# Graph network stack, layers 0 and 1: part of the layer norm on GpSimd, stores and loads on other queues, a new order of the row preparation

## The reference

```
layer 0: norm = d^-1/2 * adj.T * d^-1/2 (d = column sums of adj);  norm @ (h @ W0) + bias
layer 1: inc = adj + (adj > 0) / ||adj > 0||_row;  (inc @ h) / rowsum(inc)
layer 2: four attention heads, h @ W2; softmax(leaky_relu(src_i + dst_j) + adj), mean over the heads
layer 3: relu(adj @ (max(sign(h), 0) @ sign(W3).T))
```

## Time and profile before

| | |
|---|---|
| runs, median (lowest to highest) | 728.18 us (727.69 to 729.91) |
| the profiled execution | 727.12 us |
| its span, first to last instruction | 724.8 us |
| layer 0's products on PE | 65.6 to 149.5 us |
| layer 1's blocks on PE | 149.5 to 274.1 us |
| mean granted clock of PE | 0.995 |

### The profile page before, as it was taken

One profiled execution on the slowest core, in us unless ns is written; L12 is line 12 of the kernel. 1 busy time (PEld: TensorE's weight loads), 2 busy tenths in 40 slices (PEclk: granted clock), 3 DMA queues, 4 the chain that ended last, 5 costly groups with the idle time before them and its releaser, 6 DMA issues.

```text
span 724.8 us, 16131 instructions
## 1 busy us (share of the span) xinstructions
PE 691.0 (95%) x6480; PEld 586.1 (81%) x6480; DVE 629.4 (87%) x1161; ACT 472.4 (65%) x814; POOL 135.6 (19%) x162
## 2 busy tenths in 40 slices
PE   3998999986999999999999999999999999999998
PEld 3676888875888885468888888888888888888887
DVE  6898579688999854799999999989999899998683
ACT  3887153648887624886557867578766778667660
POOL 3962721301223220001210021200121000000000
PEclk9999999998999999999999999999999999999999
DMA  9997999677499887759988779997999831126791
GB/s 337 342 318 238 426 424 309 201 185 219 134 275 277 190 175 234 162 127 243 235 193 235 176 166 257 199 267 161 229 224 228 267 129 30 30 81 188 255 392 46
DMA packets 146457, 159.54 MB, mean 220 GB/s; under 512 B 90896, under 2 KB 103888, under 8 KB 141904
## 3 DMA queue, kind: packets, MB, share of 16 engines
q1 hardware_dynamic: 127328, 117.10, 53.7%
q0 software_dynamic: 19056, 41.42, 25.4%
HBM read 76.15 MB, written 52.46 MB: 177 GB/s over the span
## 4 chain that ended last, share of the span: by engine, by line
PE 60%; DVE 21%; ACT 6%; DMA 4%; issue 4%; SPq 2%; POOL 2%; ACTq 0%; DVEq 0%; POOLq 0%
PE ps L835 11%; PE ps L837 11%; PE ps L836 11%; DVE arena L1473 6%; PE ps L775 6%; DVE arena L1480 5%; PE ps L877 4%; PE ps L878 4%; DVE arena L1346 2%; DMA arena<-in_adj_dram 2%; SPq L383 2%; ACT arena L1003 2%; PE ps L719 2%; PE ps L721 1%; PE ps L720 1%
## 5 line engine op out<-in xcount | busy, mean ns | idle before, releaser
L835 PE MATMUL ps<-arena 128*128 128x257 f16 x1024 | 279.9, 273 | 1.0 <-DVE arena L1480 0.6
L837 PE MATMUL ps<-arena 128*128 128x257 f16 x1024 | 279.4, 273 | 0.0
L836 PE MATMUL ps<-arena 128*128 128x257 f16 x1024 | 279.2, 273 | 0.0
L1168 ACT ACTIVATE arena<-arena 128x512 f16<-128x512 f32 x252 | 158.3, 628 | 93.8 <-PE ps L837 56.3
L1473 DVE SCALAR_TENSOR_TENSOR arena<-arena,w_j 128x512 f32<-128x512 f32 x256 | 190.2, 744 | 0.0
L1480 DVE TENSOR_TENSOR arena<-arena 128x512 f16<-128x512 f32 x256 | 175.7, 687 | 8.1 <-ACT arena L1168 7.8
L835 PEld LDWEIGHTS ps<-arena 128*128 128x128 f16 x1024 | 99.9, 98 | 15.0 <-issue 1.4
L836 PEld LDWEIGHTS ps<-arena 128*128 128x128 f16 x1024 | 100.3, 98 | 12.5
L837 PEld LDWEIGHTS ps<-arena 128*128 128x128 f16 x1024 | 99.8, 97 | 12.9
L719 PE MATMUL ps<-arena 128*128 128x257 f16 x256 | 71.1, 278 | 1.9 <-DVE arena L1298 1.9
L721 PE MATMUL ps<-arena 128*128 128x257 f16 x256 | 70.5, 275 | 0.0
(11 more groups left out here) (154 smaller groups left out, 1154.9 us busy)
## 6 DMA issues: line engine op xcount, KB each, us to landing
adj_t<-arena POOLq DMA_DIRECT2D x32, 1024.0 KB, 7.9
arena<-in_adj_dram SPq DMA_DIRECT2D x32, 512.0 KB, 6.0
arena<-in_adj_dram SPq DMA_DIRECT2D x16, 1024.0 KB, 5.8
adj_parts<-arena SPq DMA_DIRECT2D x16, 1024.0 KB, 25.7
arena<-adj_t SPq DMA_DIRECT2D x64, 256.0 KB, 4.5
arena<-adj_t SPq DMA_DIRECT2D x16, 1024.0 KB, 6.7
x<-arena POOLq DMA_DIRECT2D x15, 512.0 KB, 5.7
arena<-u_rows SPq DMA_DIRECT2D x4, 1024.0 KB, 14.7
```

The source lines that it names most:

```text
L835: mm(ps[:, bank, 0:DE], hi, ht_hi[:, head, j, 0:DE], start=s, stop=False)
L836: mm(ps[:, bank, 0:DE], hi, ht_lo[:, head, j, 0:DE], start=False, stop=False)
L837: ins = mm(ps[:, bank, 0:DE], lo, ht_hi[:, head, j, 0:DE], start=False, stop=e)
L1168: nc.scalar.activation(p_hi[:, j % 4, :], prob[:, j % 4, :], copy).then_inc(p_hi_done, 1)
```

## The change

The diff, cut to its core (the lines of the new order are complete for SP, POOL, ACT and DVE in layers 0 and 1). `inc_slot` and the two functions after it only say which of three buffers a row uses; `wa_junk` gets eight buffers instead of four.

```diff
-        COUNTS = (1, 2, 9, 10, 11)
-        FILLS = (3, 4, 11, 12, 14)
-        HIGHS = (4, 7, 12, 13, 15)
-        LOWS = (5, 8, 13, 14)
+        COUNTS = (1, 2, 6, 7, 8, 11, 12)
+        FILLS = (3, 4, 8, 9, 11, 13)
+        HIGHS = (4, 6, 9, 10, 13)
+        LOWS = (5, 7, 10, 12, 14)
+        MAXIMA = 3
+        def inc_slot(t):
+            return t % 2 if t < 4 else (t - 2) % 3
...
@@ SP: while adj is read, after half 11
+                    sp.dma_start(b0_bc, b0_d.partition_broadcast(P)).then_inc(bias_in, 16)
...
             def reload_rows(t):
-                sp.wait_ge(filled, t - 2)
+                sp.wait_ge(filled, inc_last(t) + 1)
                 load_rows(t)
...
-            def turn_adj(n):
+            def turn_adj(n, part):
                 q, g = n // TG, n % TG
-                if n >= 2:
+                if n >= 2 and part == 0:
                     sp.wait_ge(wide[(n - 2) % TG], 16 * ((n - 2) // TG + 1))
...
-            sp.wait_ge(h0_lo_done, NB)
-            sp.dma_start(b0_bc, b0_d.partition_broadcast(P)).then_inc(bias_in, 16)
-            for k, (lo, hi) in enumerate(SENT):
-                for b in range(lo, hi):
-                    sp.dma_start(nat_dram[b * P:(b + 1) * P], ...).then_inc(nat_sent[k], 16)
+            reload_rows(2)
             reload_rows(3)
-            reload_rows(4)
             sp.wait_ge(y_ps, 6)
             sp.wait_ge(max_made, 7)
             sp.wait_ge(nat_sent[3], 48)
-            load_rows(2)
+            load_rows(4)
             sp.wait_ge(nat_sent[2], 32)
             turn_inc(0)
             sp.wait_ge(y_ps, 8)
+            sp.wait_ge(max_made, 9)
             turn_inc(1)
+            reload_rows(5)
+            reload_rows(6)
...
             for t in range(2, AHEAD):
-                reload_rows(t + 3)
                 sp.wait_ge(y_ps, 10 + t)
+                sp.wait_ge(max_made, 11 + t)
                 turn_inc(t)
-            for t in range(AHEAD + 3, 12):
-                reload_rows(t)
+                if t == 2:
+                    reload_rows(7)
+            reload_rows(8)
             for k in range(5):
                 sp.wait_ge(nat_sent[k], 16 * (SENT[k][1] - SENT[k][0]))
-            for n in range(2):
-                sp.wait_ge(inc_in[4 - n], 32)
-                turn_adj(n)
-            for t in range(12, NB):
-                reload_rows(t)
-            for n in range(2, QB):
-                turn_adj(n)
+            sp.wait_ge(inc_in[4], 32)
+            turn_adj(0, 0)
+            reload_rows(9)
+            turn_adj(0, 1)
+            sp.wait_ge(inc_in[3], 32)
+            turn_adj(1, 0)
+            reload_rows(10)
+            turn_adj(1, 1)
+            reload_rows(11)
+            reload_rows(12)
+            turn_adj(2, 0)
+            reload_rows(13)
+            turn_adj(2, 1)
+            reload_rows(14)
+            turn_adj(3, 0)
+            reload_rows(15)
+            turn_adj(3, 1)
...
@@ POOL
+            pool.wait_ge(bias_in, 16)
+            for t in range(NB):
+                pool.wait_ge(normed, t + 1)
+                nc.gpsimd.tensor_tensor(x[:, t, :], x[:, t, :], b0_bc, ALU.add).then_inc(bias_added, 1)
             pool.wait_ge(deg_copied, 1)
             ... dinv ...
-            (the same bias adds, after dinv)
             def inverse_root1(t):
+                pool.wait_ge(dl, CHAIN0 * (t + 1))
+                if t >= 2:
+                    pool.wait_ge(h1_lo_done, t - 1)
+                nc.gpsimd.tensor_scalar(ln_relu[:, t % 2, :], x[:, t, :], mean_var[:, t % 2, 0:1], 0.0, ALU.subtract,
+                                        ALU.max).then_inc(relu1, 1)
                 pool.wait_ge(ve1, t + 1)
                 ... power -1/2 ...
             def inverse_root2(t):
+                (the same for h2_relu, after dm and h2_lo_done)
...
                 inverse_root1(t)
-                if t in COUNTS:
-                    inverse_count(COUNTS.index(t))
+                if t - 1 in COUNTS:
+                    inverse_count(COUNTS.index(t - 1))
             for t in range(NB):
                 if t >= 1:
                     inverse_root2(t - 1)
-                if t + 5 < NB:
+                if 2 <= t and t + 5 < NB:
                     inverse_count(t + 5)
+                if t == 5:
+                    widen_high(0)
                 if t == 6:
-                    widen_high(0)
-                if t == 7:
                     add_low(0)
                     widen_high(1)
-                if t == 8:
+                if t == 7:
                     add_low(1)
-                if t == 11:
+                if t == 9:
                     widen_high(2)
-                if t == 12:
+                if t == 10:
                     add_low(2)
                     widen_high(3)
-                if t == 13:
+                if t == 11:
                     add_low(3)
...
@@ PE, layer 1
-                    if g == 3 and t == 6:
+                    if g == 3 and t == 15:
                         pe.wait_ge(wa_done, 1)
-                        for k in range(4):
+                        for k in range(NB - 2):
                             scores(k)
-                    if g == 3 and t >= 6:
-                        scores(t - 2)
...
@@ ACT
+            def send_nat(k):
+                lo, hi = SENT[k]
+                for b in range(lo, hi):
+                    nc.scalar.dma_start(nat_dram[b * P:(b + 1) * P], ...).then_inc(nat_sent[k], 16)
+            act.wait_ge(nat_lo_done, HALVES)
+            for k in range(2):
+                send_nat(k)
             ... g_hi of the 16 blocks ...
+            for k in range(2, 6):
+                send_nat(k)
...
             for t in range(NB):
                 h1_high(t)
+                if t in HIGHS:
+                    inc_high(HIGHS.index(t))
                 if t in COUNTS:
                     sign(COUNTS.index(t))
                     count(COUNTS.index(t))
-                if t in HIGHS:
-                    inc_high(HIGHS.index(t))
...                 (layer 1: sign and count from t = 2; part 3 now ahead of h2_high)
@@ DVE
+            dve.wait_ge(bias_added, NB)
             v.memset(nat_max, 0.0).then_inc(max_made, 1)
...             (layer0: no wait for bias_added, no subtraction L1323)
+            for t in range(MAXIMA):
+                maxima(t)
             for t in range(NB):
-                maxima(t)
+                if t + MAXIMA < NB:
+                    maxima(t + MAXIMA)
                 layer0(t)
...             (row_norm: no subtraction L1396)
-                if t == 0:
-                    inc_low(4)
-                if AHEAD <= t + 4 < NB:
+                if t == 1:
+                    fill(6)
+                if 3 <= t and t + 4 < NB:
                     fill(t + 4)
...
                 if t >= 1:
                     h2_low(t - 1)
-                (dot products in blocks 1 to 4, low part of W2 in blocks 5 to 8)
+                if t == 12:
+                    dve.wait_ge(w2_in, 32)
+                if t in (12, 13):
+                    w2_a(t - 12, range(HEADS))
+                if t == 14:
+                    w2_a_parts()
+                    dve.wait_ge(w2_hi_done, 1)
+                if t in (14, 15):
+                    (two of the four operations of L1435 in each)
-                if t == 12:
+                if t == 11:
                     dve.wait_ge(max_made, NB + 1)
                     v.tensor_reduce(amax[:, 0:1], nat_max, AX_X, ALU.max).then_inc(amax_part, 1)
```

More of the change, by code:

```diff
@@ L156, in gnn_stack @@
         w2_f = view(72 * KB, [DC, HD], F32)
-        wa_junk = view(80 * KB, [4, D], F32)
+        wa_junk = [view((80 + 57 * (k // 4) + k % 4) * KB, [D], F32) for k in range(2 * HEADS)]
         h2_t = view(H2T, [2 * DC, N], F16)
@@ L196, in gnn_stack @@
         SENT = ((0, 1), (1, 3), (3, 5), (5, 8), (8, 11), (11, NB))
+        CHAIN0 = 2
+        CHAIN1 = 3
         EARLY = 4
@@ L212, in gnn_stack, with inc_use, inc_last @@
         DINV_PIECES = ((0, 1), (1, 4), (4, 9), (9, NB))
+        def inc_slot(t):
+            return t % 2 if t < 4 else (t - 2) % 3
+        def inc_use(t):
+            return sum(inc_slot(k) == inc_slot(t) for k in range(t + 1))
+        def inc_last(t):
+            return max(k for k in range(t) if inc_slot(k) == inc_slot(t))
         def row_slot(t):
@@ L375, in turn_inc @@
                                            ).then_inc(inc_in[t % AHEAD], 16)
-            def turn_adj(n):
+            def turn_adj(n, part):
                 q, g = n // TG, n % TG
-                if n >= 2:
+                if n >= 2 and part == 0:
                     sp.wait_ge(wide[(n - 2) % TG], 16 * ((n - 2) // TG + 1))
                 slot = (turn_l1 if q == 0 else turn_l2)[n % 2]
[L382 to L385, removed]
+                sp.dma_start_transpose(out=slot[:, part, :, :],
+                                       in_=nat_dram[TG * P * g:TG * P * (g + 1), part, QB * P * q:QB * P * (q + 1)]
```

(19 more changed lines are left out.)

37 lines of the change are left out of this document (12 added, 25 removed).

## The result

| | us | ratio to before (95% interval) |
|---|---|---|
| before, median of 4 runs | 727.93 | |
| after, median of 4 runs (752.39 to 754.92) | 753.47 | 1.0347 (1.0319 to 1.0375) |
| predicted | 737.2 (723 to 747) | |

The account below looks back on a forecast made before the run. PE was taken to set the pace outside layers 0 and 1, where some 14 us could be won. Terms -2.3 -1.3 -3.0 +9.9 +2.6 +3.1 = +9.0 on 727.1 profiled gave 736.1, median 737.2 us (723 to 747).

Parts of the forecast that it names:

- seam and its half clock, to block 3: Between layers 0 and 1: block 2 starts 2.3 us earlier, and the half clock behind the seam is halved, -1.3.
- gaps of blocks 3 to 11: Layer 1: DVE loses the subtraction and the W2 work of blocks 1 to 8, so 3.0 us of gaps go.
- stops at the rows, half clock: Layer 1, block 9: row 13's read waits behind turn_adj(2, 0); PE stands 9.9 us, then half clock, +2.6.
- end of layer 1: Last turns of layer 1: late W2 work and POOL's subtraction make PE wait for W2, +3.1 us (+1.3 to +5.6).
- The loop itself: Layer 0's loop over 16 blocks through DVE, POOL and ACT: 5.65 us per block with a fill or split ahead.
- keeps 95.4 us as the time of block 3: Layer 0: block 3's statistics still end at 95.4 us, because ACT's first high part will not come before 85.33.
- the loop above hides even that: Layer 0: bias adds ahead of dinv may start it up to 5.8 us later, at no cost unless the seam closes.
- have this stop as cover: Layer 1: reads of rows 14 and 15, behind later turn_adj transfers, cost nothing beyond the stop at row 13.
- if POOL stands before `add_low(3)`: End of layer 1: upper bound of that term, +5.6 us against the +3.1 forecast.
- (a): Rival: row 13's stop doesn't come, the row or `wide` being there in time; 724.7 us, chance 0.14.
- (b): Rival: POOL's subtraction costs about what DVE's did, the seam closes, row 13's stop stays; 726.5 us, chance 0.16.
- (c): Rival: DVE's two-input operations shut POOL out; layer 0 starts 5.8 us late, loop 6 us a block; 751 us, chance 0.15.

Follow-up runs that it names:

- the last-but-one experiment: Kernel with rows first, subtraction on DVE and bias after dinv (717.2 us), but layer 1's subtraction on POOL again: 725.3 us, ratio 0.9944.
- the pause: Changed kernel with one wait added: in each block of layer 0 DVE waits after the variance until POOL's subtraction is done; 749.5 us, ratio 1.0263.
- the one with four parts undone: Changed kernel with rows read first, subtraction on DVE, bias after dinv and W2 work early: 718.5 us, ratio 0.9846.
- the other four: Rows first, subtraction on DVE, bias after dinv: 717.2 us; that with add_low(1) in block 8: 713.3; with layer 0's subtraction on POOL: 728.8; with layer 1's: 725.3.

## Why the prediction was wrong, step by step

The prediction's terms against the table of first products. The scores that moved (0.15 us for each block's six products, 1.6 us for the eleven that left earlier blocks, 2.0 forecast) are taken out of the blocks and of the end: +3.28 at block 3; gaps 0.9 less up to block 8 and the 1.6 us gap at 242 us gone; the stops 9.44 + 4.60 and 2.3 + 1.7 for the clock behind them; 25.96 - 17.13 - 1.6 at the end.

| term | forecast | measured | |
|---|---|---|---|
| seam and its half clock, to block 3 | -3.6 | +3.3 | failed |
| gaps of blocks 3 to 11 | -3.0 | -2.5 | right |
| stops at the rows, half clock | +12.5 | +18.0 | mechanism right, one stop missed |
| end of layer 1 | +3.1 | +7.2 | mechanism right, POOL's wait and half clock left out |
| sum | +9.0 | +26.0 | |

**The seam: the start of the loop.** The loop itself was right: from block 3 (100.07 us) to block 14 (162.40) it takes 5.67 us a block, 5.65 was forecast, and a subtraction behind a fill takes 3.3, forecast 2.3 + 0.9. (In four of the five blocks with a split it is the power that is held up, not the subtraction.) What failed is the sentence that keeps 95.4 us as the time of block 3 because ACT's first high part would not come sooner. The price of the bias adds stood beside it, up to 5.8 us (measured 5.80), and was dismissed with "the loop above hides even that". That sum put 5.8 us on PE's end of layer 0 alone. But the loop is fed by PE's first block: a late layer 0, with its half clock, delays the loop as well, and block 3 came 4.7 us late. ACT's stores, the reason that was given for 85.33, are issued behind the high parts of `g` and so come late with layer 0 too: ACT's first high part came at 89.27, and at 89.00 with the subtraction on DVE. The other failure is to have seen the adds and the subtractions as two edits. Both are POOL's: behind `dinv` the adds slow DVE, whose statistics the first subtraction needs (85.00 us), ahead of it they hold up layer 0. Only without the subtraction does moving them pay in full (8.6 against 1.5 us).

**The stops.** The first was right in place, chain and size: 9.44 us, forecast 9.9, from `add_low(0)` landing 7.7 us after its issue (8.7 forecast) and the row 6.1 after its own (5.8). The step that failed is "reads 14 and 15 stand behind `turn_adj(2, 1)` and `(3, 0)`, but have this stop as cover". The cover is 9.4 us; what row 14 lost was 6.12 us of SP and 13.7 us to land. Such a landing was in the rows (17.2 at most) and was left out as a matter of the stores; here none of those was in flight. It made a stop of 4.60 and twice the half clock: 2.3 + 1.7 us instead of 2.6. With the subtraction on DVE the second stop is 0.84 us, and the row lands in 10.6 us; whether POOL's subtraction slows the transfers was not separated.

**The end of layer 1.** The chain was right, and the larger bound (+5.6 "if POOL stands before `add_low(3)`") named what happened: POOL stood 5.23 us, DVE then 1.90 us for the high part, and layer 2's first product is 5.5 us late, the scores taken out. The forecast took this as a bound. The other 1.7 us are the half clock of layer 2's first twelve products, for which the sum had no term. It takes two things to make the end long, POOL's subtraction and the late W2 work: undoing the one gains 3.9 us there (4.4 by the last-but-one experiment), undoing the other 5.8 without the scores, and with the subtraction on DVE the W2 work may stand early or late. The sentence that POOL's subtraction in layer 1 "has cover" failed too: 3.7 us in blocks 0 to 10 once the covering losses are gone.

**The rivals.** (a) and (b) are out: the stops came, the subtraction cost 2.36 us in layer 0's mean. (c) was the case, at 0.15: POOL shut out, layer 0 5.8 us late, 751 against the median of 753.5. That its total came so close is in part luck: its loop of 6 us was too long, it hid the late start behind that loop, it had one stop for two, and it kept the small gaps, of which 2.5 us went. The argument against it, the median of 1.72 us, came from work that held up PE by 0.2 us in all; the duration that counts is the one at the moment when POOL's input is ready, which is when DVE starts its next long operation.

(c)'s rule, in the Trainium skill on SBUF — State Buffer, section SBUF: two separate sides, is an exclusive lock between GpSimd and a DVE instruction with two SBUF inputs: the one that starts first holds it for the whole instruction. This case agrees where DVE starts with POOL or before it: 3.31 us beside a fill of 2.35, 1.15 beside an operation that takes one input from PSUM, 1.15 throughout with the pause. Where POOL has started first it agrees in part: DVE's split pays 0.5 us beside a bias add (1.75 instead of 1.23), its maximum 0.2 beside a subtraction that it overlaps for 1.03 us, and the split that starts 0.65 us into a subtraction nothing (2.29, 2.28 in the mean with the subtraction on DVE). (b)'s rule, on the GPSIMD Engine Reference, section Engine selection (one-input operations at roughly line rate), does not hold here: undisturbed the subtraction takes 1.14 us on POOL against 0.34 on DVE.

## What to carry to other kernels

Work moved from DVE to POOL is priced by what DVE starts at that moment, not by POOL's idle time: here a DVE operation on two SBUF tensors stopped POOL until it ended, and POOL's operation cost DVE 0 to 0.5 us. A stage that starts late also starts the loop that was to hide it; carry the delay to every input of the loop, not only to its end. In an ordered list of transfers a read must not stand behind one that waits for another engine: the rows ahead of such transfers were worth 14.8 us.

## What the runs showed of the hardware

- A read of 1 MB that lands in 4.9 us at the least needed 13.7 us with an accumulating store and a transposing read in flight, and 10.6 in the same place with the subtraction on DVE; which of them made it so is open.
- PE's granted clock was 0.50 from 60 to 77 us in the changed kernel, behind a stretch with many gaps of up to 0.67 us. With the bias adds behind `dinv` it was still 0.50 from 60 to 64 us in the kernel with that edit alone (behind one wait of 1.35 us), 0.71 in the one with four parts undone, and 1.00 in the other four; what decides is open.
